# Long attention: pieces of the maxima that take every seventh query, and reciprocals one round later

## The reference

```python
scores = jnp.einsum('bhsr,bhlr->bhsl', q_r, k_r)     # 16 heads x 56 queries = 896 rows, 1500 keys
attn = jax.nn.softmax(scores, axis=-1)
ctx_c = jnp.einsum('bhsl,bld->bhsd', attn, kv_rope)
```

## Time and profile before

| | |
|---|---|
| median of 3 runs | 2405.49 us (2403.42 to 2409.81) |
| profiled execution, its own time | 2404.89 us |
| its span, first to last instruction | 2403.1 us |
| mean granted TensorE clock | 0.938 of full speed |
| busy share of the span | PE 92%, DVE 61%, POOL 47%, ACT 40% |

### The profile page before, as it was taken

How to read it: one execution, slowest core, us unless ns; L and a number is a source line. 1 busy time by engine, 2 the same in 40 slices (tenths; PEclk the granted TensorE clock), 3 DMA queues, 4 the chain that set the end, 5 groups by cost and what they waited for, 6 DMA issues and landing times. The chain is left out here.

```text
span 2403.1 us, 37321 instructions
## 1 busy us (share of the span) xinstructions
PE 2208.8 (92%) x13148; PEld 1532.7 (64%) x13148; DVE 1469.7 (61%) x2468; ACT 958.9 (40%) x1433; POOL 1125.4 (47%) x612
## 2 busy tenths in 40 slices
PE   6768998989999998897999999899799999998998
PEld 4447997745555557664555555698365555567997
DVE  2765444277777756787777775412677777745444
ACT  1443443334445451212454445111345445533443
POOL 0331332037777770363777777011067777731332
PEclk9878998789999998997999999879799999998999
DMA  4473631365464513124545542286755544402332
GB/s 81 138 247 92 214 122 51 87 176 113 105 135 105 124 39 123 43 92 111 131 103 116 125 102 60 61 292 265 199 122 113 120 109 109 103 9 94 121 120 80
DMA packets 123792, 285.54 MB, mean 119 GB/s; under 512 B 33282, under 2 KB 76028, under 8 KB 119721
## 3 DMA queue, kind: packets, MB, share of 16 engines
q1 hardware_dynamic: 122984, 281.96, 44.0%
q0 software_dynamic: 672, 1.84, 0.2%
HBM read 237.15 MB, written 46.41 MB: 118 GB/s over the span
## 5 line engine op out<-in xcount | busy, mean ns | idle before, releaser
L1226 DVE TENSOR_REDUCE keep_top<-banks 128x1 f32<-128x500 f32 x945 | 603.2, 674 | 242.7 <-PE banks L1150 238.5
L1296 ACT ACTIVATE att_ex<-banks 125x896 f32<-125x896 f32 x576 | 524.5, 919 | 241.0 <-PE banks L1143 222.0
L1175 PE MATMUL banks<-att_ex,att_v 125*64 125x448 f32 x2304 | 464.8, 545 | 0.0
L1349 POOL TENSOR_TENSOR att_acc<-att_acc,att_ex 125x896 f32<-125x896 f32 x186 | 391.4, 2104 | 130.4 <-ACT att_ex L1296 116.8
L1150 PE MATMUL banks<-keep_kh,keep_qt 64*128 64x500 f32 x1008 | 364.6, 449 | 31.1 <-PEq L574 10.7
L1349 POOL TENSOR_TENSOR att_acc<-att_acc,att_two 125x896 f32<-125x896 f32 x141 | 296.6, 2103 | 118.0 <-DVE att_two L1238 118.0
L1175 PEld LDWEIGHTS banks<-att_ex,att_v 125*64 125x64 f32 x2304 | 152.5, 136 | 246.9 <-issue 182.9
L1143 PE MATMUL banks<-att_ql,keep_kh 64*125 64x448 f32 x1152 | 299.1, 366 | 0.0
L1143 PE MATMUL banks<-att_sh,att_on 64*125 64x448 f32 x1152 | 297.4, 365 | 0.0
L1664 PE MATMUL banks<-moe_xs,moe_w 128*128 128x448 f32 x1272 | 278.8, 369 | 5.3 <-DVE moe_w L1760 3.7
L1238 DVE TENSOR_TENSOR att_two<-att_ex 125x896 f32<-125x896 f32 x144 | 235.9, 1638 | 62.9 <-ACT att_ex L1296 56.8
(11 more groups left out here) (271 smaller groups left out, 2761.4 us busy)
## 6 DMA issues: line engine op xcount, KB each, us to landing
keep_kh<-kvt_hi SPq DMA_DIRECT2D x96, 375.0 KB, 5.1
att_kl<-kvt_lo SPq DMA_DIRECT2D x96, 375.0 KB, 7.1
q_rows<-mats_q SPq DMA_DIRECT2D x24, 896.0 KB, 4.4
keep_qt<-q_rows SPq DMA_DIRECT2D x96, 224.0 KB, 5.8
moe_raw<-L_experts_dram SPq DMA_DIRECT2D x53, 384.0 KB, 4.1
att_v<-kvn SPq DMA_DIRECT2D x24, 720.0 KB
sort_wu<-L_experts_dram SPq DMA_DIRECT2D x14, 1024.0 KB, 10.1
moe_cb<-comb_rows SPq DMA_DIRECT2D x62, 224.0 KB
```

Of the source, the lines that this page charges most:

```text
L1175: last = pe.matmul(PS[WEIGHED][64 * e:64 * e + 64, 0:HALF], v[:, s // 2, u, s % 2, :], ex[:, u % RING, e, :], start=u == 0, stop=u == UNIT ...
L1226: dve.tensor_reduce(top[:, s % 2, n // NS, n % NS:n % NS + 1], PS[6 + (PIECES * s + n) % 2][:, 0:SB], AX.X, ALU.max).then_inc(mx_done, 1)
L1296: act.activation(ex[:, u % RING], scored, ACT.Exp).then_inc(exp_done, 1)
L1349: pool.tensor_tensor(a, a if n else ex[:, 0], two[:, i] if k == 2 else ex[:, k], ALU.add).then_inc(gathered, 1)
```

## The change

The tiles of the maxima take every seventh query: tile t is t, t + 7, t + 14 and so on, so that `nm[p, t]` belongs to query 7p + t, and `nm` read partition by partition is already in the order of `sh`. `turn` and `high` go, with PE's waits on them. The four DMAs of `shifts` become two, each of 64 runs of 7 elements. `nm` is written by DVE in the reduced type that `nmh` had, and DVE's `shift` waits until the DMAs of two batches ago have read it.

DVE's `invert` moves from behind the pair of round 1 to ahead of the pair of round 2. SP issues `scales(b - 1)` behind `shifts(b + 1)`, not ahead of it. POOL's `place` moves from batch b, round 2 (for b - 1) to batch b + 1, round 0 (still for b - 1, written as `place(b - 2)`).

```diff
 def shifts(b):
-    s = b % 2
-    sp.wait_ge(high_done, b + 1)
-    for e, at, tiles, a, z in ((0, 0, (0, 3), 0, 128), (0, 384, (3, 4), 0, 64),
-                               (1, 0, (3, 4), 64, 128), (1, 64, (4, NT), 0, 128)):
-        n = (tiles[1] - tiles[0]) * (z - a)
-        sp.dma_start(sh[64 * e:64 * e + 1, s, at:at + n].rearrange("o (t p) -> o t p", p=z - a).bitcast(FP32),
-                     nmh[tiles[0]:tiles[1], s, a:z].bitcast(FP32)).then_inc(m_in[s], 16)
+    sp.wait_ge(nm_ready, b + 1)
+    for e in range(2):
+        rows = slice(64 * e, 64 * e + 64)
+        sp.dma_start(sh[64 * e:64 * e + 1, b % 2, :].rearrange("o (p t) -> o p t", t=NT).bitcast(FP32),
+                     nm[rows, b % 2, :].bitcast(FP32)).then_inc(m_in[b % 2], 16)
...
     if b:
         sums(b - 1)
-        scales(b - 1)
     if b < B - 1:
         shifts(b + 1)
+    if b:
+        scales(b - 1)
...
 def maxima(bank, s, n, half):
-    return pe.matmul(PS[bank][:, 0:SB], q[rows, s, 128 * t:128 * t + 128],
+    return pe.matmul(PS[bank][:, 0:SB], q[rows, s, t:t + NT * 127 + 1:NT],
                      kh[rows, s, SB * c:SB * c + SB], start=True, stop=True)
...
-def turn(s, b):
-    pe.wait_ge(nm_ready, b + 1)
-    if not known(b, 2):
-        pe.wait_ge(sm_done, b - 1)
-    pe.matmul(PS[SUMMED][0:NT, 0:128], nm[:, s % 2, :], G["ident"][:, :],
-              start=True, stop=True).then_inc(nt_ready, 1)
...
 if i == 0 and not known(b, 1):
     pe.wait_ge(gathered, GATHERS * b)
-    pe.wait_ge(high_done, b + 1)
     sums([acc[:, (s + 1) % 2]])
-if i == 1 and left:
-    turn((s + 1) % 4, b + 1)
...
 def shift(s, b):
     dve.wait_ge(mx_done, PIECES * b + PIECES)
+    if not known(b, 2):
+        dve.wait_ge(m_in[s % 2], of_two(s, b - 2, 32))
...
+if i == ROUNDS - 1 and not known(b, 1):
+    invert(s + 1, b - 1)
 if i == ROUNDS - 1 and not left:
     last_pair(b)
 pair(b, i)
-if i == 1 and not known(b, 1):
-    invert(s + 1, b - 1)
...
-def high(s, b):
-    act.wait_ge(nt_ready, b + 1)
-    if not known(b, 2):
-        act.wait_ge(m_in[s % 2], of_two(s, b - 2, 64))
-    act.activation(nmh[:, s % 2, :], PS[SUMMED][0:NT, 0:128],
-                   ACT.Copy).then_inc(high_done, 1)
...
-if i == ROUNDS - 1 and k == 1 and b:
-    place(b - 1)
+if i == 0 and k == 2 and b > 1:
+    place(b - 2)
```

More of the change, by code:

```diff
@@ L994, in attend_long @@
     with Stage(nc, f"att{l}") as st:
-        kh, q, top, nm, nmh = (G[n] for n in ("kh", "qt", "top", "nm", "nmh"))
+        kh, q, top = (G[n] for n in ("kh", "qt", "top"))
+        nm = st.sb("nm", [128, 2, NT], F32R)
         kl = st.sb("kl", [128, 2, L], F32R)
@@ L1007, in attend_long @@
             st.sem(n) for n in ("ones", "st_ready", "exp_done", "pv_done", "mx_ready", "mx_done", "paired", "gathered"))
-        nm_ready, nt_ready, high_done, cu_done, sums_ready, sm_done, sum_out, sum_in, inverted, rs_out, placed = (
-            st.sem(n) for n in ("nm_ready", "nt_ready", "high_done", "cu_done", "sums_ready", "sm_done", "sum_out",
+        nm_ready, cu_done, sums_ready, sm_done, sum_out, sum_in, inverted, rs_out, placed = (
+            st.sem(n) for n in ("nm_ready", "cu_done", "sums_ready", "sm_done", "sum_out",
                                 "sum_in", "inverted", "rs_out", "placed"))
@@ L1139, in score @@
                     if u == 0 and part == 3:
-                        pe.wait_ge(m_in[s % 2], of_two(s, b, 64))
+                        pe.wait_ge(m_in[s % 2], of_two(s, b, 32))
                     for e in (first, 1 - first):
@@ L1211, in _ @@
                     last.then_inc(mx_ready, NS)
-                turn(0, 0)
                 for n in range(NT):
@@ L1322, in batch @@
                             row_sums(b - 1)
-                        if i == 1 and left:
-                            high((s + 1) % 4, b + 1)
                     if left:
                         numerators(s, b)
-                high(0, 0)
                 emit(act, batch)
```

## The result

| | median of 6 runs | range |
|---|---|---|
| before | 2403.34 us | 2401.51 to 2409.81 |
| after | 2414.09 us | 2410.43 to 2416.54 |

The ratio is 1.0037, 95% interval 1.0022 to 1.0052: slower, where I forecast 2382.0 and faster. The profiled execution took 2415.89 us, its span is 2414.1.

A forecast was written before the change was run, and what follows sets the result against it. The prediction took each round's chain of PE and ACT work, with PE nearly always busy, as the bound. Savings of 14.0 + 1.6 + 7.9 = 23.5 us, with strided loads free, gave a median of 2382.0 us, range 2376 to 2436.

The forecast's parts named there:

- The strided weights: PE's piece loads of columns 28 bytes apart: taken as costing nothing, upper bound 55 us.
- Half rate: Rival: strided loads take 0.22 us instead of 0.11, costing 20 us, giving 2402 us; chance 0.21.
- break-even of 0.18 us a round: Loss per round with pieces beyond which strided loads outweigh the gains: 23.5 us over 132 rounds.
- much slower: Rival: strided loads take up to 335 ns, costing 55 us, giving 2437 us; chance 0.23.
- the case that I thought likeliest: No penalty on strided loads: 2377 to 2390 us, chance 0.47.
- The turning: PE's turn between `weigh` and the next round's pieces: removing 0.31 us in 45 batches saves 14.0 us.
- the reciprocals: DVE's wait at `invert` for late sums in batches that load values: moving it saves 7.9 us, at least 4.
- the heads' 1.6: Three turnings at the heads of the layers delay the following pieces by 0.53 us each: 1.6 us saved.
- another wait takes the turning's place: Rival, with no earlier round start: a bank or exponential holds the round, only 7.9 us remain, 2397 us; chance 0.05.
- The moves at nothing: Moved `invert`, `place`, shift DMAs and later next-batch loads in SP's queue: all covered, costing nothing.
- no earlier start: Rival: rounds do not start earlier without the turning, only the reciprocals' 7.9 us are left, 2397 us; chance 0.05.
- wait moves along: Rival: DVE's wait moves with `invert`, so that move gains nothing; 15.6 us are left, 2390 us; chance 0.04.

The follow-up runs named there:

- a1: The changed kernel with the pieces of the maxima loading 128 adjacent queries again, the layout unchanged: 2384.85 us, ratio 0.9895.
- s1: The changed kernel with tiles 0 to 6 loading their columns at steps of 1 to 7, each on its own line: 2394.23 us, one execution.
- p1: The changed kernel with a round's first two pieces moved behind the first and second product of the scores: 2413.55 us, ratio 1.0018.
- b2: The kernel before with the reciprocals' part of the change alone (`invert`, SP's order and `place` moved): 2395.69 us, ratio 0.9938.
- t1: The changed kernel with adjacent weights and the reciprocals' part undone, leaving only the removed turning: 2403.42 us, ratio 0.9972.
- n1: The changed kernel with adjacent weights, the maxima put in order by eight DMAs of 64 or 128 single elements: 2385.87 us, ratio 0.9903.

## Why the prediction was wrong

**The step that failed** is in "The strided weights": "I take nothing, since the load reads only half as fast as the product beside it". A load of columns 28 bytes apart takes about 0.20 us of PE in place of 0.11. It costs about 30 us (a1: 29.5 within the copies alone), more than the 23.5 us of all gains. The reason I gave compared the load with another kind of reading and took unused rate for room. That the load's rate hangs on adjacent columns was open, and the row that would have told it was not in the trace of before. What the Trainium skill says in "Advanced Engine Details and Errata", section "SBUF Cachelines", agrees with s1: steps 1 and 2, where two columns or more share 16 bytes, read 183 and 191 ns, and from step 4 on it is 299 to 308. I had it beside my sum and gave it less weight than an argument of my own.

**The size.** "Half rate" was the right kind, 0.20 for 0.11 us, but its 20 us were too small: 0.24 us a round on average, not 0.15, that is 132 x 0.24 = 32 us. At the round's start 0.13 (1.48 - 1.35) was lost, near the 0.11 forecast. The other 0.18 us lies between unit 2's start and `weigh` (2.45 for 2.27), where three pieces stand, 0.06 each, and I had priced two of them at 0.02 and the third at nothing. Their loads too stand behind running products, so the picture of cover fails there, though it nearly holds for the two pieces that p1 moved. By my own break-even of 0.18 us a round the rival "much slower" won, although the time came out nearer to the half rate's 2402 than to its 2437. Its bound, "over 0.25 us in place of 0.11", mixed two scales: 0.25 follows from the record (0.335 - 0.184 = 0.15 at the start), where the load now reads 0.307, while 0.11 is PE's own time for a load, which is now 0.20. Its sign that DVE waits more for pieces is there, weakly: 86.9 us against 77.8 in the first long layer. The range held the result (2414.09 in 2376 to 2436) only because it was stretched to take in the rivals; the case that I thought likeliest ended at 2390.

**The turning and the reciprocals** were right together. Sum forecast 23.5 us; a1 measured 1035.8 - 1014.1 = 21.7 in the spans, which leave out the heads' 1.6 and some first and last rounds. Its median is 2384.85 for 2382, and 25.5 under the kernel before on its own chip. The reciprocals alone are 7.8 (b2) for 7.9. The turning is 1028.0 - 1014.1 = 13.9 on top of them (a1 against b2), for 42 of its 45 rounds (13.0 by the forecast). What the prediction did not see is that the turning's 14.0 can't be had alone (t1). There the rival "another wait takes the turning's place" came true, with the reciprocals' wait, which I had not named. The two parts are not a sum of independent terms: the second frees the first.

**The moves at nothing** held: a1, which has all of them, spans the forecast's 338 us a layer. DVE never waits in `invert`. `place` got shorter, 1156 ns where it was 2.00 us, and waits for its broadcast only 3 times:

```profile
L1338 POOL TENSOR_TENSOR ctx_ctxT<-att_cu,att_rsb x45: 1143/1156/1777, 569.4 to 2142.8; 128x448 f32<-128x448 f32 x45
...
  DMA att_rsb<-rs_rows: 8.3, 3
```

In the change itself the rivals "no earlier start" and "wait moves along" did not come: in the first long layer a round that opens with pieces starts 3.15 or 3.16 us behind `weigh`, and b2 brought its 7.8 us.

## What to carry to other kernels

A view that drops a transposition moves its price to every instruction that reads through it: count those first (1008 strided loads here, against 48 turnings), and treat a load whose step no trace shows as unpriced, not as free. Where two or more of the columns share each 16 bytes, at step 1 or 2 in 4-byte elements, a load takes 183 or 191 ns; if an order must be mended, do it where it happens once a batch, as n1 does with slow but mostly hidden DMAs (5 us over a1). And test parts both alone and together: one that starts work earlier may only wait longer for a transfer until another has moved that wait.

## What the runs showed of the hardware

- A weight load of 128 fp32 columns on 64 partitions takes 183, 191, 249 and 299 to 308 ns on record at steps 1, 2, 3 and 4 to 7. From 64 stretches of 16 bytes on, each 32 more add 57 or 58 ns (191 to 249 to 306).
- Such a load can cost time behind a running product of 0.20 us as well: from unit 2's start to `weigh`, with three such loads, a round outside the loop takes 2.45 us in place of 2.27. At a round's start a product covered it nearly: 1.38 us to the first exponential (p1), against 1.48 without one and 1.35 with adjacent loads. What makes the difference is not shown.
- POOL's product of 128 x 448 fp32 took 1156 ns in its new place, where before, in the earlier trace rows, it took 2.00 us. In both kernels that keep the old place (before, t1) the median is 2.00 us, in b2 and the change, which move it, 1.16. In the old place of the earlier trace rows DVE's `pair`, which also reads two tensors in SBUF, runs from 605.98 to 608.00, and `place` ends 1.01 us after it; no run here isolates the cause.
- SP took 5.0 to 6.3 us to issue eight DMAs of 64 or 128 single elements, and 1.14 us for two of 64 runs of 28 bytes, which landed 1.8 us after their issue (median).
